# Linear attention in a Trainium2 transformer layer: the normalisation of the query-times-KV product, moved from VectorE to ScalarE and VectorE together

## The chip, the cores and the metric

The kernel runs on all 8 cores of one Trainium2 chip. There are four batch items of 2048 tokens, and each core does one half of one item (1024 tokens). All 8 cores run the same program. The metric is the device time of the slowest core in microseconds (us).

## What is computed

One layer: linear attention with a residual and a layernorm, then a mixture of 8 experts with a residual and a layernorm. The change lies in the attention:

```python
sq = elu_plus_one(q)                                # 16 heads of 128
sk = elu_plus_one(k)                                # 4 KV heads, each repeated for 4 query heads
kv = jnp.einsum('bhsd,bhse->bhde', sk, v)           # 128x128 per head
qkv = jnp.einsum('bhsd,bhde->bhse', sq, kv)
k_sum = sk.sum(axis=2)
norm = jnp.einsum('bhsd,bhd->bhs', sq, k_sum)
attn = qkv / (norm[..., None] + EPS)                # EPS = 1e-6
return attn.transpose(0, 2, 1, 3).reshape(b, s, H * D) @ Wo.T
```

## The kernel before

The program is written by hand, stage by stage. Each stage is one `nc.Block` with a function for each engine. The engines of a block run side by side, ordered only by semaphores that the code names (`wait_ge`, `then_inc`); at the end of a block all engines meet. The stages are: init, kpass (K projection), vpass (V projection and the product of K and V), qproj (Q projection), qkv, wo (output projection), ln1, routerdown, the experts, and then the up projection, the core projection and the last layernorm.

The change touches qkv (lines 583 to 639). It makes 128 tiles, 16 heads by 8 tiles of 128 tokens. For tile i:

- **Q(i)**, TensorE, line 592: a matmul of the 128x128 query tile with `kvaug`, the 128x128 product of K and V with one more column, the sum of K. The result, 128x129 in a PSUM bank `pb[i % 4]`, holds the unnormalised attention in columns 0 to 127 and the norm in column 128.
- **add**, VectorE, line 622: norm + EPS into `rc[4]`, 128x1. It is wrapped in `chain` (line 202), which lets the engine wait for the semaphore of its own instruction.
- **R(i)**, VectorE, line 625: reciprocal into `rc[5]`, 128x1, in `chain` too.
- **M(i)**, VectorE, line 626: columns 0 to 127 times the reciprocal, into `tbx[i % 2]`, bf16.
- **T(i)**, TensorE, line 602 (line 610 for the last two): transpose of `tbx` into `pbf[i % 2]`, the bf16 view of the PSUM bank `pbx`. It waits for M(i), and for the copy C(i-2).
- **C(i)**, VectorE, line 633 (637 for the last): copy of the transposed tile into its place in `arC`, from which wo reads. It waits for one transpose more than its own, so C(i-1) waits for T(i).

The order on TensorE is Q(i+2), T(i), Q(i+3), T(i+1) and so on. The order on VectorE is add(i), R(i), M(i), C(i-1), add(i+1). Semaphore `mma` counts the matmuls, `mmb` the transposes, `dva` the scalings (by two, since a `nop` counts as well), `dvb` the copies and `dvs` the steps of `chain`. ScalarE, GpSimd and SyncE have no work in this stage.

Around it: the stage qproj ends with the epilogues of lines 557 (ScalarE, relu with a per-partition bias from PSUM), 568 (VectorE), 561 (ScalarE, exp) and 572 (VectorE); line 331 is the same relu without a bias, in kpass. Stage wo streams Wo: SyncE issues the loads at line 489, ScalarE casts each piece to bf16 with a Copy activation at line 510, and TensorE multiplies at line 533. The query projection uses the same function and so the same lines. Line 1037 is a Copy activation in the experts, lines 868 and 873 are small activations in the router, lines 722 and 737 are a Square activation and the matmul behind it in ln1. L1282, in a later stage, is a transpose like T.

Of the kernel before, what the change touches and what calls it, by code (L numbers as in the profile page):

```python
# [6 lines left out]
F32 = mybir.dt.float32  # L7
# [55 lines left out]
def build_nc():  # L63
# [43 lines left out]
    def sb(name, shape, dt):  # L107
        return stx.enter_context(nc.sbuf_tensor(name, list(shape), dt))
# [63 lines left out]
    phg = sb("phg", (128, 64), BF16)  # L172
    rbc = sb("rbc", (8, 1), F32)
    ncc = sb("ncc", (8, 1), F32)
    idb = sb("idb", (128, 128), BF16)
    id8 = sb("id8", (8, 8), F32)
    onr = sb("onr", (1, 128), BF16)
# [24 lines left out]
    def chain(eng, instr, ctr):  # L202
        instr.then_inc(ctr.h, 1)
        ctr.add(1)
        eng.wait_ge(ctr.h, ctr.v)  # L205
# [3 lines left out]
    try:  # L209
        with nc.Block("init") as blk:  # L210
# [50 lines left out]
            @blk.vector  # L261
            def _(v):
                v.memset(kvaug[:], 0.0)
                chain(v, v.memset(rc[0][:, 0:1], 1.0), dvs)
                chain(v, v.reciprocal(rc[1][:, 0:1], rc[0][:, 0:1]), dvs)
                chain(v, v.reciprocal(rc[1][:, 0:1], rc[0][:, 0:1]), dvs)
                for jc in range(NJ):
                    v.wait_ge(ldx2[0].h, 16 * (jc + 1))
                    v.tensor_copy(xtb(jc)[:, 0:1024], w2st[0][:, :]
                                  ).then_inc(dvs.h, 1)  # L270
                    dvs.add(1)
                    v.wait_ge(ldx2[1].h, 16 * (jc + 1))
                    v.tensor_copy(xtb(jc)[:, 1024:2048], w2st[1][:, :]
                                  ).then_inc(dvs.h, 1)
                    dvs.add(1)
                v.wait_ge(dvs.h, dvs.v)
                v.nop().then_inc(dva.h, 1)
                dva.add(1)
# [302 lines left out]

        _ck(4)
        with nc.Block("qkv") as blk:
            mma_b, mmb_b, dva_b, dvb_b = mma.v, mmb.v, dva.v, dvb.v

            @blk.tensor
            def _(te):
                for i in range(128):
                    h, ti = i // NT1, i % NT1
                    if i >= 4:  # L590
                        te.wait_ge(dva.h, dva_b + 2 * (i - 4) + 2)
                    te.matmul(pb[i % 4][:, 0:129],
                              sqv(h)[:, ti * 128:(ti + 1) * 128],
                              kvaug[:, (h // 4) * 130:(h // 4) * 130 + 129],
                              start=True, stop=True).then_inc(mma.h, 1)
                    mma.add(1)
                    if i >= 2:
                        k = i - 2
                        te.wait_ge(dva.h, dva_b + 2 * k + 2)
                        if k >= 2:  # L600
                            te.wait_ge(dvb.h, dvb_b + k - 1)
                        te.transpose(pbf[k % 2][:], tbx[k % 2][:, 0:128],  # L602
                                     idb[:]).then_inc(mmb.h, 1)
                        mmb.add(1)
                te.drain().then_inc(mma.h, 1)
                mma.add(1)
                for k in (126, 127):
                    te.wait_ge(dva.h, dva_b + 2 * k + 2)
                    te.wait_ge(dvb.h, dvb_b + k - 1)
                    te.transpose(pbf[k % 2][:], tbx[k % 2][:, 0:128], idb[:]  # L610
                                 ).then_inc(mmb.h, 1)
                    mmb.add(1)
                te.drain().then_inc(mmb.h, 1)
                mmb.add(1)

            @blk.vector
            def _(v):
                for i in range(128):
                    v.wait_ge(mma.h, mma_b + min(i + 3, 129))
                    v.nop().then_inc(dva.h, 1)  # L620
                    dva.add(1)
                    chain(v, v.tensor_scalar(rc[4][:, 0:1],
                                             pb[i % 4][:, 128:129],
                                             EPS_ATTN, None, ALU.add), dvs)
                    chain(v, v.reciprocal(rc[5][:, 0:1], rc[4][:, 0:1]), dvs)
                    v.tensor_scalar(tbx[i % 2][:, 0:128], pb[i % 4][:, 0:128],  # L626
                                    rc[5][:, 0:1], None, ALU.mult).then_inc(dva.h, 1)
                    dva.add(1)
                    if i >= 1:
                        k = i - 1  # L630
                        h, ti = k // NT1, k % NT1
                        v.wait_ge(mmb.h, mmb_b + min(k + 2, 129))
                        v.tensor_copy(atv(h)[:, ti * 128:(ti + 1) * 128],
                                      pbf[k % 2][:]).then_inc(dvb.h, 1)
                        dvb.add(1)
                v.wait_ge(mmb.h, mmb_b + 129)
                v.tensor_copy(atv(15)[:, 7 * 128:8 * 128], pbf[127 % 2][:]
                              ).then_inc(dvb.h, 1)
                dvb.add(1)

        dump("attnT", bfv(arC)[:, 0:16384], (128, 16384), BF16)
        dump("qdbg", stg[:, 0:512], (128, 512), F32)
# [834 lines left out]
```

## Time and profile before

| | us |
|---|---|
| two timed runs | 3197.44 and 3456.91, median 3327.17 |
| profiled execution | 3207.53 |
| its slowest core (core 0), first to last instruction | 3206.0 |
| the other cores of that execution | 3156.3 to 3195.6 |
| busy in the span: TensorE / weight loads / VectorE / ScalarE / GpSimd | 2110.3 / 873.9 / 708.0 / 804.1 / 279.0 |

All 8 cores ran at a mean granted TensorE clock between 0.845 and 0.852 of full speed. Times in the profile are from the start of the span. A "granted clock" of 1.0 is 2.4 GHz, 0.5 is 1.2 GHz. In a view, `[0.62 <-PE pbx L602]` behind an instruction means that its engine sat idle 0.62 us before it, and that the last thing it waited for was TensorE's write to pbx at line 602.

### The profile page before, as it was taken

The numbers are of one execution on the slowest core, as the hardware profiler recorded it, in microseconds if no ns is written. First come the engines' busy times: TensorE is split into PE (matmuls) and PEld (weight loads), VectorE is DVE, ScalarE is ACT, GpSimd is POOL, SyncE is SP. The second block draws the span as 40 slices with busy tenths as digits, with TensorE's granted clock in tenths as the row PEclk, the third lists the DMA queues.
The fourth block names the chain that finished last, engine by engine and source line by source line (L and its number), as shares of the span: only waits on it lengthen the run. The fifth ranks groups of instructions, "written<-read, shape, count | busy, mean of one in ns | idle before, by whom it ended". The sixth has DMA issues, their size and how long they took to land. (4 is left out here: it accounts for less than half of the span.)

```text
span 3206.0 us, 29912 instructions; the slowest of 8 cores (3156.3 to 3206.0 us)
## 1 busy us (share of the span) xinstructions
PE 2110.3 (66%) x8759; PEld 873.9 (27%) x8926; DVE 708.0 (22%) x1553; ACT 804.1 (25%) x1371; POOL 279.0 (9%) x724
## 2 busy tenths in 40 slices
PE   0258673225843708888888888888888887737981
PEld 0023231112300303333333333333333333303420
DVE  2121224551135021111111111111111111230116
ACT  0130441003341232222222222222222222124341
POOL 1000000000000001111111111111111111000000
PEclk9989885557966859899999999999999999858985
DMA  4310330004502113334443333333333333104412
GB/s 153 112 53 1 112 95 4 1 1 143 166 7 59 47 33 116 110 119 124 122 118 114 118 112 106 105 106 105 105 105 106 105 105 124 54 14 136 129 38 105
DMA packets 213226, 287.48 MB, mean 90 GB/s; under 512 B 27713, under 2 KB 179265, under 8 KB 213068
## 3 DMA queue, kind: packets, MB, share of 16 engines
q1 hardware_dynamic: 206156, 260.39, 26.9%
q0 software_dynamic: 6912, 25.17, 2.5%
q8 instruction: 76, 1.25, 0.2%
q14 instruction: 82, 0.67, 0.1%
HBM read 277.08 MB, written 8.39 MB: 89 GB/s over the span
## 5 line engine op out<-in xcount | busy, mean ns | idle before, releaser
L1060 PE MATMUL pb<-arE,wsl 128*128 128x512 bf16 x1771 | 459.5, 412 | 229.1 <-POOL wsl L1011 161.1
L1081 PE MATMUL pb<-arB,arF 128*128 128x512 bf16 x1753 | 403.1, 379 | 27.0 <-ACT arF L1028 25.2
L1011 POOL CAST wsl<-stg 128x256 bf16<-128x256 f32 x672 | 253.5, 400 | 1607.7 <-DMA stg<-w 1420.8
L1142 DVE SCALAR_TENSOR_TENSOR arC<-pb,wgt,arC 128x512 f32<-128x512 f32 x203 | 151.8, 751 | 788.5 <-PE pbx L1081 410.6
L1060 PEld LDWEIGHTS pb<-arE,wsl 128*128 128x128 bf16 x1792 | 181.3, 104 | 493.6 <-issue 327.2
L1028 ACT ACTIVATE arF<-pb,b1all 128x512 bf16<-128x512 f32 x224 | 151.5, 682 | 644.8 <-PE pbx L1060 331.9
L1060 PE MATMUL pbx<-arE,wsl 128*128 128x512 bf16 x861 | 232.8, 413 | 73.9 <-POOL wsl L1011 37.3
L1081 PEld LDWEIGHTS pb<-arB,arF 128*128 128x128 bf16 x1792 | 174.2, 98 | 238.7 <-issue 30.5
L1037 ACT ACTIVATE arB<-w2st 128x1024 bf16<-128x1024 f32 x168 | 176.7, 1052 | 175.3 <-DMA w2st<-w 169.0
L1081 PE MATMUL pbx<-arB,arF 128*128 128x512 bf16 x879 | 209.4, 379 | 12.9 <-ACT arF L1028 12.0
L1028 ACT ACTIVATE arF<-pbx,b1all 128x512 bf16<-128x512 f32 x112 | 76.5, 683 | 345.6 <-PE pb L1060 336.1
L533 PE MATMUL pb<-arA,wsl 128*128 128x512 bf16 x501 | 126.3, 415 | 54.9 <-DVE arB L572 38.1
L1142 DVE SCALAR_TENSOR_TENSOR arC<-pbx,wgt,arC 128x512 f32<-128x512 f32 x101 | 75.8, 751 | 369.9 <-PE pb L1081 364.0
L1373 PE MATMUL pb<-arC,wsl 128*128 128x512 bf16 x500 | 122.9, 398 | 51.8 <-ACT wsl L1335 39.9
L349 PE MATMUL pb<-wsl,arA 128*128 128x512 bf16 x251 | 59.6, 389 | 140.8 <-ACT wsl L324 140.6
L1060 PEld LDWEIGHTS pbx<-arE,wsl 128*128 128x128 bf16 x896 | 91.1, 104 | 204.4 <-issue 121.2
L602 PE MATMUL pbx<-idb,tb 128*128 128x128 bf16 x126 | 33.5, 266 | 171.7 <-DVE tb L626 171.7
L533 PE MATMUL pb<-arC,wsl 128*128 128x512 bf16 x501 | 116.4, 392 | 38.0 <-ACT wsl L510 36.2
L510 ACT ACTIVATE wsl<-stg 128x256 bf16<-128x256 f32 x256 | 98.6, 413 | 125.2 <-DMA stg<-wot 78.5
L1081 PEld LDWEIGHTS pbx<-arB,arF 128*128 128x128 bf16 x896 | 87.1, 98 | 119.4 <-issue 15.3
L533 PEld LDWEIGHTS pb<-arA,wsl 128*128 128x128 bf16 x512 | 53.3, 105 | 127.6 <-issue 78.3
L1373 PEld LDWEIGHTS pb<-arC,wsl 128*128 128x128 bf16 x512 | 51.7, 102 | 118.4 <-issue 64.4
(152 smaller groups left out, 1539.7 us busy)
## 6 DMA issues: line engine op xcount, KB each, us to landing
stg<-w SPq DMA_DIRECT2D x640, 128.0 KB, 3.6
w2st<-w SPq DMA_DIRECT2D x160, 512.0 KB, 4.8
w2st<-xt POOLq DMA_DIRECT2D x48, 512.0 KB, 4.8
stg<-wqt SPq DMA_DIRECT2D x128, 128.0 KB, 2.5
stg<-wot SPq DMA_DIRECT2D x128, 128.0 KB, 3.0
stg<-core_w SPq DMA_DIRECT2D x128, 128.0 KB, 2.6
stg<-down_w SPq DMA_DIRECT2D x64, 128.0 KB, 2.5
w2st<-up_w SPq DMA_DIRECT2D x64, 128.0 KB, 2.5
```

The costliest lines, as they stand in the source:

```text
L349: te.matmul(pb[s_ % 4][:, 0:512], xtb(jc)[:, s_ * 128:(s_ + 1) * 128], wslv(jc // 8)[:, (jc % 8) * 512:(jc % 8) * 512 + 512], start=(jc == ...
L510: sc.activation(wslv(osl % 2)[:, ic * 256:(ic + 1) * 256], stgv(np_), AF.Copy).then_inc(aca.h, 1)
L533: mm = te.matmul(pb[i % 4][:, 0:512], wslv(osl % 2)[:, ic * 256 + k2 * 128: ic * 256 + k2 * 128 + 128], rhs_fn(ic, th), start=(ic == 0), s ...
L602: te.transpose(pbf[k % 2][:], tbx[k % 2][:, 0:128], idb[:]).then_inc(mmb.h, 1)
L1011: gp.tensor_copy(wslv(sg % 2)[:, lc * 256:(lc + 1) * 256], stgv(npiece)).then_inc(gpc.h, 1)
L1028: sc.activation(Uv(hcl)[:, th * 512:th * 512 + 512], eb1[ztg % 3][:], AF.Gelu, bias=b1all[:, bcol:bcol + 1]).then_inc(acb.h, 1)
L1037: sc.activation(w2g(zt)[:, :], w2st[kc % 2][:, :], AF.Copy).then_inc(aca.h, 1)
L1060: mm = te.matmul(eb1[ztg % 3][:, 0:512], wslv(sg % 2)[:, lc * 256 + k2 * 128: lc * 256 + k2 * 128 + 128], gTv(lc)[:, th * 512:th * 512 + 512],
L1081: mm = te.matmul(eb2[mtg % 3][:, 0:512], Uv(hcl)[:, ti * 128:(ti + 1) * 128], w2g(hcl)[:, lh * 512:lh * 512 + 512], start=(hcl == 0), stop ...
L1142: fl = v.scalar_tensor_tensor(dst, eb2[mtg % 3][:], wgt[:, ti * 8 + g["e"]: ti * 8 + g["e"] + 1], dst, ALU.mult, ALU.add)
L1373: te.matmul(pb[i % 4][:, 0:512], wslv(osl % 2)[:, jc * 256 + k2 * 128: jc * 256 + k2 * 128 + 128], gx2v(jc)[:, th * 512:th * 512 + 512], s ...
```

## The change

In qkv the add of EPS and the scaling M move from VectorE to ScalarE, as Copy activations: the add with EPS as an immediate bias, M with the reciprocal as a per-partition scale. The reciprocal stays on VectorE.

- ScalarE's order is N(i), M(i-1), N(i+1), M(i) and so on, where N is the add. N(i) waits for matmul Q(i+1) and then for R(i-2), whose input buffer it overwrites. M(k) waits for transpose T(k-2) and then for R(k).
- VectorE's order is R(i), C(i-1), R(i+1), C(i). R(i) waits for N(i) and then for M(i-2), whose scale it overwrites. The self-waits of `chain` and the `nop` are gone.
- `rc[4]` and `rc[5]` (sums) and `rc[2]` and `rc[3]` (reciprocals) are each used in turn.
- TensorE does what it did; it waits for the scaling on `acb` (ScalarE) in place of `dva`.
- The last copy becomes part of the loop. A 128x1 constant `epsc` is set in init and is not read.

```diff
@@ -172,6 +172,7 @@
     phg = sb("phg", (128, 64), BF16)
     rbc = sb("rbc", (8, 1), F32)
     ncc = sb("ncc", (8, 1), F32)
+    epsc = sb("epsc", (128, 1), F32)
     idb = sb("idb", (128, 128), BF16)
     id8 = sb("id8", (8, 8), F32)
     onr = sb("onr", (1, 128), BF16)
@@ -261,6 +262,7 @@
             @blk.vector
             def _(v):
                 v.memset(kvaug[:], 0.0)
+                v.memset(epsc[:, 0:1], EPS_ATTN)
                 chain(v, v.memset(rc[0][:, 0:1], 1.0), dvs)
                 chain(v, v.reciprocal(rc[1][:, 0:1], rc[0][:, 0:1]), dvs)
                 chain(v, v.reciprocal(rc[1][:, 0:1], rc[0][:, 0:1]), dvs)
@@ -581,14 +583,14 @@
 
         _ck(4)
         with nc.Block("qkv") as blk:
-            mma_b, mmb_b, dva_b, dvb_b = mma.v, mmb.v, dva.v, dvb.v
+            mma_b, mmb_b, dvb_b, acb_b = mma.v, mmb.v, dvb.v, acb.v
 
             @blk.tensor
             def _(te):
                 for i in range(128):
                     h, ti = i // NT1, i % NT1
                     if i >= 4:
-                        te.wait_ge(dva.h, dva_b + 2 * (i - 4) + 2)
+                        te.wait_ge(acb.h, acb_b + (i - 4) + 1)
                     te.matmul(pb[i % 4][:, 0:129],
                               sqv(h)[:, ti * 128:(ti + 1) * 128],
                               kvaug[:, (h // 4) * 130:(h // 4) * 130 + 129],
@@ -596,7 +598,7 @@
                     mma.add(1)
                     if i >= 2:
                         k = i - 2
-                        te.wait_ge(dva.h, dva_b + 2 * k + 2)
+                        te.wait_ge(acb.h, acb_b + k + 1)
                         if k >= 2:
                             te.wait_ge(dvb.h, dvb_b + k - 1)
                         te.transpose(pbf[k % 2][:], tbx[k % 2][:, 0:128],
@@ -605,7 +607,7 @@
                 te.drain().then_inc(mma.h, 1)
                 mma.add(1)
                 for k in (126, 127):
-                    te.wait_ge(dva.h, dva_b + 2 * k + 2)
+                    te.wait_ge(acb.h, acb_b + k + 1)
                     te.wait_ge(dvb.h, dvb_b + k - 1)
                     te.transpose(pbf[k % 2][:], tbx[k % 2][:, 0:128], idb[:]
                                  ).then_inc(mmb.h, 1)
@@ -613,19 +615,40 @@
                 te.drain().then_inc(mmb.h, 1)
                 mmb.add(1)
 
+            acs_b, dva_b = acs.v, dva.v
+
+            @blk.scalar
+            def _(sc):
+                for i in range(129):
+                    if i < 128:
+                        sc.wait_ge(mma.h, mma_b + min(i + 2, 129))
+                        if i >= 2:
+                            sc.wait_ge(dva.h, dva_b + i - 1)
+                        sc.activation(rc[4 + i % 2][:, 0:1],
+                                      pb[i % 4][:, 128:129], AF.Copy,
+                                      bias=EPS_ATTN).then_inc(acs.h, 1)
+                        acs.add(1)
+                    if i >= 1:
+                        k = i - 1
+                        if k >= 2:
+                            sc.wait_ge(mmb.h, mmb_b + k - 1)
+                        sc.wait_ge(dva.h, dva_b + k + 1)
+                        sc.activation(tbx[k % 2][:, 0:128],
+                                      pb[k % 4][:, 0:128],
+                                      AF.Copy, scale=rc[2 + k % 2][:, 0:1]
+                                      ).then_inc(acb.h, 1)
+                        acb.add(1)
+
             @blk.vector
             def _(v):
-                for i in range(128):
-                    v.wait_ge(mma.h, mma_b + min(i + 3, 129))
-                    v.nop().then_inc(dva.h, 1)
-                    dva.add(1)
-                    chain(v, v.tensor_scalar(rc[4][:, 0:1],
-                                             pb[i % 4][:, 128:129],
-                                             EPS_ATTN, None, ALU.add), dvs)
-                    chain(v, v.reciprocal(rc[5][:, 0:1], rc[4][:, 0:1]), dvs)
-                    v.tensor_scalar(tbx[i % 2][:, 0:128], pb[i % 4][:, 0:128],
-                                    rc[5][:, 0:1], None, ALU.mult).then_inc(dva.h, 1)
-                    dva.add(1)
+                for i in range(129):
+                    if i < 128:
+                        v.wait_ge(acs.h, acs_b + i + 1)
+                        if i >= 2:
+                            v.wait_ge(acb.h, acb_b + i - 1)
+                        v.reciprocal(rc[2 + i % 2][:, 0:1],
+                                     rc[4 + i % 2][:, 0:1]).then_inc(dva.h, 1)
+                        dva.add(1)
                     if i >= 1:
                         k = i - 1
                         h, ti = k // NT1, k % NT1
@@ -633,10 +656,6 @@
                         v.tensor_copy(atv(h)[:, ti * 128:(ti + 1) * 128],
                                       pbf[k % 2][:]).then_inc(dvb.h, 1)
                         dvb.add(1)
-                v.wait_ge(mmb.h, mmb_b + 129)
-                v.tensor_copy(atv(15)[:, 7 * 128:8 * 128], pbf[127 % 2][:]
-                              ).then_inc(dvb.h, 1)
-                dvb.add(1)
 
         dump("attnT", bfv(arC)[:, 0:16384], (128, 16384), BF16)
         dump("qdbg", stg[:, 0:512], (128, 512), F32)
```

## Rows read from the trace of the kernel before

**Rows 1.** The page: the span, and the TensorE clock granted in 40 slices.
```profile
span 3206.0 us, 29912 instructions; the slowest of 8 cores (3156.3 to 3206.0 us)
...
PEclk9989885557966859899999999999999999858985
```

**Rows 2.** Stretches, core 0: us, busy PE, PEld, DVE, ACT, POOL, granted clock, DMA.
```profile
512.00:734.00 222.00, 49.63 (x251) 25.96 (x250) 113.25 (x505) 0.00 (x0) 0.00 (x0) 0.50 0.00 1
737.00:760.00 23.00, 3.88 (x12) 1.68 (x14) 0.00 (x0) 9.80 (x23) 0.55 (x2) 0.52 0.61 178
2817.00:2864.00 47.00, 16.84 (x64) 6.61 (x64) 18.87 (x78) 0.00 (x0) 0.00 (x0) 0.50 0.00 1
```

**Rows 3.** Waits of SyncE's queue, 500 to 745 us: total, times, longest.
```profile
SPq L583 <- PEq L583: 226.0, 1, 226.0
```

**Rows 4.** Timeline, one tile of qkv: start us, us, engine, line, operation, idle before.
```profile
603.67 0.23 DVE L633 COPY arC<-pbx 128x128 bf16<-128x128 bf16 x1 [0.62 <-PE pbx L602]
603.89 0.16 DVE L622 TENSOR_SCALAR rc<-pb 128x1 f32<-128x1 f32 x1
604.16 0.16 DVE L625 RECIPROCAL rc<-rc 128x1 f32<-128x1 f32 x1
604.43 0.35 DVE L626 TENSOR_SCALAR tb<-pb,rc 128x128 bf16<-128x128 f32 x1
605.00 0.10 PEld L602 LDWEIGHTS pbx<-idb,tb 128*128 128x128 bf16 x1 [1.50 <-issue]
605.03 0.27 PE L602 MATMUL pbx<-idb,tb 128*128 128x128 bf16 x1 [1.34 <-DVE tb L626]
...
605.16 0.27 PE L592 MATMUL pb<-kvaug,arB 128*128 128x129 bf16 x1
605.40 0.23 DVE L633 COPY arC<-pbx 128x128 bf16<-128x128 bf16 x1 [0.62 <-PE pbx L602]
```

**Rows 5.** Timeline, the first tile of qkv.
```profile
511.14 0.35 DVE L626 TENSOR_SCALAR tb<-pb,rc 128x128 bf16<-128x128 f32 x1
511.61 0.10 PEld L602 LDWEIGHTS pbx<-idb,tb 128*128 128x128 bf16 x1 [1.48 <-issue]
```

**Rows 6.** Timeline, the end of qkv and the start of wo.
```profile
734.94 0.10 PEld L610 LDWEIGHTS pbx<-idb,tb 128*128 128x128 bf16 x1 [1.60 <-issue]
...
735.97 9.17 SPq L489 DMA_DIRECT2D stg<-wot  x8
...
738.37 1.28 ACT L510 ACT_TABLE_LOAD   x1 [229.57 <-DMA stg<-wot]
```

**Rows 7.** Groups of ScalarE: line, operation, shapes, count, busy us, mean ns, idle before.
```profile
L1037 ACT ACTIVATE arB<-w2st 128x1024 bf16<-128x1024 f32 x168 | 176.7, 1052 | 175.3 <-DMA w2st<-w 169.0 <-DMA w2st<-shared_w 6.3
...
L510 ACT ACTIVATE wsl<-stg 128x256 bf16<-128x256 f32 x256 | 98.6, 413 | 125.2 <-DMA stg<-wot 78.5 <-DMA stg<-wqt 40.1 <-PE pb L533 3.7
...
L557 ACT ACTIVATE tscr<-pb,bqs 128x512 f32<-128x512 f32 x32 | 21.6, 675 | 20.2 <-PE pb L533 19.0 <-PEq L545 1.2
...
L331 ACT ACTIVATE tscr<-pb 128x512 f32<-128x512 f32 x16 | 9.5, 596 | 34.7 <-PE pb L353 32.9 <-PEq L358 1.8
L510 ACT ACT_TABLE_LOAD x2 | 2.6, 1283 | 317.3 <-DMA stg<-wot 229.6 <-DMA stg<-wqt 87.7
...
L868 ACT ACTIVATE rt<-rt,rc 128x8 f32<-128x8 f32 x8 | 2.4, 300 | 0.1
...
L873 ACT ACTIVATE rc<-rc 128x1 f32<-128x1 f32 x8 | 1.5, 186 | 0.0
```

**Rows 8.** Timeline, query projection: ScalarE waits for VectorE.
```profile
501.69 0.75 DVE L568 TENSOR_SCALAR tscr<-pb,bqs 128x512 f32<-128x512 f32 x1 [1.19 <-ACT tscr L557]
502.54 0.63 ACT L561 ACTIVATE tscr<-tscr 128x512 f32<-128x512 f32 x1 [0.95 <-DVE tscr L568]
```

**Rows 9.** Timeline, first layernorm: TensorE waits for ScalarE.
```profile
895.68 0.61 ACT L722 ACTIVATE tscr<-arA 128x512 bf16<-128x512 f32 x1
...
896.41 0.08 PEld L737 LDWEIGHTS pb<-tb,onc 128*1 128x1 bf16 x1 [1.31 <-issue]
```

## The prediction

> **What bounds the kernel now.** I read the page first. The core shown ends at 3206.0 us, and in slices 7 to 9 of 40 (80 us each) the granted TensorE clock is 0.5 of full speed [rows 1]. That is the stage called qkv. The view of stretches says what happens there: from 512 to 734 us VectorE is busy 113 of 222 us, TensorE 50, ScalarE and GpSimd nothing, no data is loaded, and the clock stands at 0.50, the 1.2 GHz level [rows 2]. No engine is full, so something must go round in a ring.
>
> Next, is the stage joined to its neighbours, or closed? The queue of SyncE, which loads the next stage's weights, stands 226.0 us at the end-of-stage synchronisation of qkv (line 583) [rows 3]. The first load of Wo is issued at 735.97, 1.0 us after the last transpose has begun [rows 6]. Nothing of wo is done ahead, so each microsecond taken from qkv should leave the whole kernel. (The whole-kernel chain of waits is no help, as it only follows the end.)
>
> Now one tile in the timeline [rows 4]. The reader should see the following ring, in us from the start of the copy at 603.67:
>
> - copy C of an older transpose, VectorE, 0.225, with the add of EPS starting as it ends (603.89);
> - the add takes 0.16, but the reciprocal starts 0.27 after the add did, since it waits 0.10 for its own engine's semaphore;
> - the scaling starts 0.27 after the reciprocal and takes 0.35, to 604.78;
> - the weight load of the transpose T starts 0.22 later (605.00);
> - the next copy starts 0.40 after that weight load (605.40).
>
> The sum is 0.22 + 0.27 + 0.27 + 0.35 + 0.22 + 0.40 = 1.73 us, and C to C is 605.40 - 603.67 = 1.73. The matmul Q, issued behind T at 605.16, is not in the ring. The first transpose loads at 511.61 [rows 5], the last at 734.94 [rows 6]: 223.3 us for 127 steps, or 1.758 each. 127 steps of 1.73 are 219.7, so 3.6 us are irregular stalls, which I leave in.
>
> **The change part by part.**
>
> *The EPS constant in init.* One 128x1 memset, which nothing reads. In init VectorE waits for the DMA of x; the cost is nil, and some 0.1 us even without that cover.
>
> *The add moves to ScalarE (call it N).* N(i+2) reads the bank of Q(i+3), which TensorE issues right behind T(i). So the add runs beside the copy, one to two tiles ahead of the scaling it serves. VectorE's chain loses the add and the self-wait: 0.27.
>
> *The scaling moves to ScalarE (M).* Its duration there has no row, so from neighbours [rows 7]: a PSUM read of 512 columns takes 596 ns without a pointer operand (line 331) and 675 with one (line 557). The slope is (1052 - 413)/768 = 0.832 ns per column. 128 columns with a pointer are 675 - 384 x 0.832 = 355 ns, against 0.35 on VectorE: no gain and no loss. For N, 596 - 511 x 0.832 = 171 ns; the 128x1 row of line 873 has 186. I take 0.18. The bounds: M at 0.28 if the pointer is free (596 - 384 x 0.832) and 0.40 if all PSUM savings vanish; N from 0.17 to 0.30 (line 868, 128x8 with a pointer).
>
> A rule of the Trainium skill speaks against both moves: page "ScalarE: Activation LUTs", section "Rules for kernel authors", says to do adds and multiplies on VectorE and not on ScalarE. The rows do not bear it out for this shape, since 0.355 stands against 0.35. By that page's section "What ACT_TABLE_LOAD costs" (186 ns, 93 for a pointer operand, 0.833 per column) M would be 0.386, an estimate; the ring below would then be 1.49 and the time some 4 us higher than mine.
>
> *The hand-overs.* VectorE to ScalarE: line 568 ends at 501.69 + 0.75 = 502.44 and line 561 starts at 502.54, so 0.10 [rows 8]. ScalarE to TensorE: line 722 ends at 896.29 and the weight load starts at 896.41, so 0.12 [rows 9]. VectorE to TensorE in qkv is 0.12 for the first tile, too (511.49 to 511.61) [rows 5], and 0.22 in the steady state [rows 4], where T waits for two semaphores (from k = 2 on). The new code keeps the two waits in the same order, so I take 0.22.
>
> *The new ring A:* M(i) 0.355, to TensorE 0.22, T to C(i-1) 0.40, C 0.225, reciprocal R(i+1) 0.16 directly behind it, to ScalarE 0.10, M(i+1). Sum 1.46. R's two waits (N(i+1), M(i-1)) are over by then, and so is M's wait for T(i-1).
>
> *The new ring B:* M(i) 0.355, to TensorE 0.22, T and Q(i+3) to the end of Q 0.43 (605.00 to 605.16 + 0.27), to ScalarE 0.20 (two waits, the late one first: 0.10 more, as for T), N(i+2) 0.18, and M(i+1) directly behind it on ScalarE. Sum 1.385. N(i+2) is over 0.08 before R(i+1) lets M go, so ring A sets the pace, narrowly.
>
> *Queued behind the waits.* On VectorE R(i+1) stands behind C(i-1), on ScalarE M(i+1) behind N(i+2), on TensorE Q(i+3) behind T(i); all are in the two rings. No DMA queue is touched.
>
> *ScalarE's first activation of the stage.* ScalarE does nothing in qkv now. Each of the two stages that use line 510 begins with a table load of 1.28 us (256 activations in all, but only 2 loads) [rows 7]. The wo stage keeps its load (738.37) [rows 6]. qkv gets one more. Two matmuls are done about 510.3 (the first three end by 510.40, a little before VectorE begins), the table is there at 511.7, then N 0.18, hop 0.10, R 0.16, hop 0.10, M 0.355, hop 0.12: first T at about 512.7 in place of 511.61 [rows 5]. That costs 1.1.
>
> The same skill page and section count another 1.38 us of drain to each switch of table. No row here isolates it; by it the start would cost 2.5.
>
> *The end.* The last copy is now one of the loop's, waiting for the same drain: nil.
>
> *Sum.* 127 steps x (1.73 - 1.46) = 34.3 saved, 1.1 paid: 33 us. The profiled execution took 3207.53 us (span 3206.0 and 1.5 around it), so 3207.5 - 33 = 3174.5, rounded to 3175. The two timed runs were 3197.44 and 3456.91, a median of 3327.17; the profiled execution stands 10 us above the first and far below the median, which is the midpoint of two runs 8% apart. My number is for an execution like the profiled one. From 3197.44 the same sum gives 3164.
>
> **The rivals.**
>
> *ScalarE becomes the bound (ring B).* With N at 0.30 and 0.10 more between N and M, because M has two waits of its own, ring B is 1.385 + 0.12 + 0.10 = 1.605. Saved: 127 x 0.125 = 16, less 1.1: 3193. For it: ring B lies only 0.08 below A, and ScalarE now has two instructions and four waits per tile. Against: consecutive activations without a hand-over have idle 0.0 between them (line 873) [rows 7].
>
> *The steps are shorter than I think.* M at 0.28 and T free of its second wait's 0.10: ring A 1.29, but ring B then 1.385 - 0.075 - 0.10 = 1.21, so 1.29: 127 x 0.44 = 56, less 1.1: 3153. Each alone gives 9 to 13 us more than my sum. The clock could rise to its 2.4 GHz level as TensorE gets denser (50/222 = 23% busy now, 50/189 = 26% then). Against: from 2817 to 2864 us the same transposes ran at 16.84/47 = 36% busy with the clock at 0.50 throughout [rows 2].
>
> *It does not reach the end.* If wo could not start earlier, because something other than qkv gates it, the time is 3207 to 3209. Against: the loads wait at the stage's end and start right behind it [rows 3, 6]. wo runs at the 0.52 clock from 737 to 760 whenever it begins [rows 2].
>
> *Slower: a table load at more than the first activation.* Should ScalarE reload its table within the loop, each load lies in ring A or B at 1.28. The gain of 33 is gone from 26 loads on, and one per tile gives 127 x 1.28 = 163 more, 3338. For it: ScalarE has never run such an instruction pair here. Against: both activations use one function, and line 510's 256 activations, alternated in the query projection with two other functions, show 2 loads.
>
> **How the numbers follow.** Ring A as summed (3165 to 3185): 0.62. Ring B or dearer hand-overs (3185 to 3203): 0.19. Shorter steps (3145 to 3165): 0.11. No effect: 0.05. Slower by reloads: 0.03. The predicted time is that of the first, 3175. The range is 3145 to 3212: it reaches down to the short bound less the 10 us by which an execution may lie below the profiled one, and up to no effect. 2% of 3207 is 64 us, about what a measurement of this kernel can tell from no change. A gain of 64 needs a step of 1.22, below both rings: 0.03. Slower by over 2% needs the reloads: 0.04 with what I have not thought of. Within 2%: 0.93.
>
> **What would show it.** In the changed profile: qkv from its first transpose to its last 127 x 1.46 + 3.6 = 189 us, not 223; the steady step 1.46; M about 0.355 and N about 0.18; M started by the reciprocal (ring A) and not directly at N's end (ring B); one table load at about 510.3; clock 0.50; Wo's first load at about 703. I am wrong if M's releaser is N or if the step lies outside 1.39 to 1.60, or if the stretch is shorter but the stages behind it longer.

## The result, and the profile after

The changed kernel takes 0.9898 of the time of the kernel before (95% interval 0.9864 to 0.9933). Executions in which a whole die runs at a lower clock are left out on both sides, here and below. Of 3207 us that is 33 us less, and the interval runs from 21 to 44. Its profiled execution took 3202.04 us.

The page of the changed kernel, its span and its granted clock by slice:

```profile
span 3200.5 us, 30331 instructions; the slowest of 8 cores (3111.0 to 3200.5 us)
...
PEclk9989886559868769779999999999999977858985
```

The span is only 5.5 us shorter than before [rows 1], because the slowest core of this execution lost time elsewhere. The first row below is core 0 of the kernel before, the second core 1 of the changed kernel, each from its first to its last expert matmul. The columns are those of rows 2.

```profile
1195.00:2783.00 1588.00, 1318.63 (x5584) 560.28 (x5696) 253.88 (x372) 388.67 (x505) 250.43 (x664) 0.94 0.37 110
```

```profile
1161.30:2786.00 1624.70, 1372.99 (x5695) 571.62 (x5696) 253.92 (x372) 388.61 (x505) 250.23 (x664) 0.91 0.35 108
```

The experts' code is the same, and so is the busy time of VectorE and ScalarE, but this stretch ran at a clock of 0.91 in place of 0.94 and took 1624.7 us in place of 1588.0. That is 37 us in a stretch in which no line was changed. Over all 8 cores it did not grow: its median was 1573.6 us before and is 1572.1 now. What is left of a core's span without it had a median of 1613.3 us and has 1574.8, 38.5 less, and the median of the 8 whole spans went from 3188.9 to 3145.2 us. So I read the stage itself, and its length from the first to the last transpose is the number to go by. It was 223.2 to 223.3 us on the 8 cores before, and is 182.7 to 183.1 now.

One tile of qkv in the changed kernel, timeline. L656 is the copy C, L649 the reciprocal R, L627 the add N on ScalarE, L636 the scaling M on ScalarE, L604 the transpose T and L594 the matmul Q:

```profile
602.11 0.22 DVE L656 COPY arC<-pbx 128x128 bf16<-128x128 bf16 x1 [1.08 <-PE pbx L604]
602.28 0.17 ACT L627 ACTIVATE rc<-pb 128x1 f32<-128x1 f32 x1 [0.79 <-PE pb L594]
602.29 0.16 DVE L649 RECIPROCAL rc<-rc 128x1 f32<-128x1 f32 x1
602.54 0.37 ACT L636 ACTIVATE tb<-pb,rc 128x128 bf16<-128x128 f32 x1
603.13 0.10 PEld L604 LDWEIGHTS pbx<-idb,tb 128*128 128x128 bf16 x1 [1.19 <-issue]
...
603.26 0.10 PEld L594 LDWEIGHTS pb<-kvaug,arB 128*128 128x128 bf16 x1
603.29 0.27 PE L594 MATMUL pb<-kvaug,arB 128*128 128x129 bf16 x1
603.53 0.22 DVE L656 COPY arC<-pbx 128x128 bf16<-128x128 bf16 x1 [1.08 <-PE pbx L604]
```

Set beside [rows 4], the ring now runs copy (602.11), reciprocal (602.29), scaling (602.54), weight load of the transpose (603.13), next copy (603.53): 0.18 + 0.25 + 0.59 + 0.40 = 1.42 us. The add (602.28) runs at the same time as the reciprocal of another tile, and the ring no longer contains it.

The stage without its start and end, columns as in rows 2, and its largest waits between 530 and 690 us, columns as in rows 3:

```profile
520.00:700.00 180.00, 49.42 (x250) 25.76 (x250) 41.72 (x248) 67.15 (x251) 0.00 (x0) 0.50 0.00 1
```

```profile
DVE arC L656 <- PE pbx L604: 122.1, 111, 1.4
PE pbx L604 <- ACT tb L636: 116.1, 111, 1.4
ACT rc L627 <- PE pb L594: 88.1, 110, 0.9
```

VectorE is busy a quarter of the time, and waits for a transpose; TensorE waits for the scaling; ScalarE's adds wait for a matmul. It is still a ring, with no full engine, at the 0.50 clock [rows 2].

The start of the stage (against rows 5) and its end (against rows 6):

```profile
518.63 1.28 ACT L627 ACT_TABLE_LOAD   x1 [1.57 <-PE pb L594]
519.92 0.23 ACT L627 ACTIVATE rc<-pb 128x1 f32<-128x1 f32 x2
520.20 0.26 DVE L649 RECIPROCAL rc<-rc 128x1 f32<-128x1 f32 x2 [2.35 <-ACT rc L627]
520.46 0.37 ACT L636 ACTIVATE tb<-pb,rc 128x128 bf16<-128x128 f32 x1 [0.30 <-DVE rc L649]
520.94 0.10 PEld L604 LDWEIGHTS pbx<-idb,tb 128*128 128x128 bf16 x1 [2.55 <-issue]
```

```profile
703.95 0.10 PEld L612 LDWEIGHTS pbx<-idb,tb 128*128 128x128 bf16 x1 [1.32 <-issue]
...
704.99 7.18 SPq L491 DMA_DIRECT2D stg<-wot  x7
...
707.27 1.28 ACT L512 ACT_TABLE_LOAD   x1 [3.54 <-DMA stg<-wot]
```

One table load comes before the first add. The first transpose follows the stage's first matmul by 2.8 us in place of 1.7. At the end, the loads for wo begin 1.0 us after the last transpose, as before.

### The profile page after: what moved, and what is told of

Read it like the earlier page. It is cut to its first block and busy times, and to the rows that moved or that the text cites. A ratio compares the mean times of both kernels' runs of the same rounds, so it can differ in the third digit from the quotient of the medians.

```text
span 3200.5 us, 30331 instructions; the slowest of 8 cores (3111.0 to 3200.5 us)
## 1 busy us (share of the span) xinstructions
PE 2157.9 (67%) x8926; PEld 883.4 (28%) x8926; DVE 636.4 (20%) x1298; ACT 873.7 (27%) x1628; POOL 278.8 (9%) x724
## 3 DMA queue, kind: packets, MB, share of 16 engines
q8 instruction: 76, 1.25, 0.2%
## 5 line engine op out<-in xcount | busy, mean ns | idle before, releaser
L1079 PE MATMUL pb<-arE,wsl 128*128 128x512 bf16 x1792 | 469.0, 418 | 213.1 <-POOL wsl L1030 153.8
L1100 PE MATMUL pb<-arB,arF 128*128 128x512 bf16 x1792 | 425.2, 392 | 24.0 <-ACT arF L1047 24.0
L1079 PE MATMUL pbx<-arE,wsl 128*128 128x512 bf16 x896 | 245.4, 424 | 75.2 <-POOL wsl L1030 38.5
L1100 PE MATMUL pbx<-arB,arF 128*128 128x512 bf16 x896 | 220.9, 391 | 12.0 <-ACT arF L1047 12.0
L351 PE MATMUL pb<-wsl,arA 128*128 128x512 bf16 x256 | 60.7, 392 | 144.3 <-ACT wsl L326 144.3
L604 PE MATMUL pbx<-idb,tb 128*128 128x128 bf16 x126 | 33.5, 266 | 132.9 <-ACT tb L636 132.9
L422 PE MATMUL pb<-wsl,arA 128*128 128x512 bf16 x256 | 60.3, 390 | 34.7 <-ACT wsl L409 34.7
```

What stands on the lines that cost most here:

```text
L351: te.matmul(pb[s_ % 4][:, 0:512], xtb(jc)[:, s_ * 128:(s_ + 1) * 128], wslv(jc // 8)[:, (jc % 8) * 512:(jc % 8) * 512 + 512], start=(jc == ...
L422: te.matmul(pb[s_ % 4][:, 0:512], xtb(jc)[:, s_ * 128:(s_ + 1) * 128], wslv(jc // 8)[:, (jc % 8) * 512:(jc % 8) * 512 + 512], start=(jc == ...
L604: te.transpose(pbf[k % 2][:], tbx[k % 2][:, 0:128], idb[:]).then_inc(mmb.h, 1)
L1079: mm = te.matmul(eb1[ztg % 3][:, 0:512], wslv(sg % 2)[:, lc * 256 + k2 * 128: lc * 256 + k2 * 128 + 128], gTv(lc)[:, th * 512:th * 512 + 512],
L1100: mm = te.matmul(eb2[mtg % 3][:, 0:512], Uv(hcl)[:, ti * 128:(ti + 1) * 128], w2g(hcl)[:, lh * 512:lh * 512 + 512], start=(hcl == 0), stop ...
```

## The experiments

All lengths below are from the first to the last transpose of the stage (127 steps), in us. The cores of one execution differ by 0.5 at most; the median core is given. "Step" is the median time from one transpose to the next. In e8 the steps swing, so their mean is given there.

| kernel | first to last transpose | step |
|---|---|---|
| before | 223.3 | 1.73 |
| changed | 183.0 | 1.42 |
| e1, e11: only the add on ScalarE | 176.5 | 1.38 |
| e2: only the scaling on ScalarE | 215.1 | 1.68 |
| e3: before, without the nop | 208.8 | 1.64 |
| e4: changed, waits of the transpose in the other order | 169.1 | 1.31 |
| e5: changed, reciprocal ahead of the copy | 167.6 | 1.31 |
| e6: changed, one more activation per tile | 183.3 | 1.42 |
| e7: changed, three more | 184.1 | 1.42 |
| e9: changed, one wait at the reciprocal | 178.1 | 1.38 |
| e10: only the add, and waits as in e4 | 162.5 | 1.27 |
| e8: changed, deeper | 77.8 | 0.61 |
| e12: only the add, deeper | 70.6 | 0.53 |

### Each half of the change alone (e1, e2)

For e1, the scaling stays on VectorE and ScalarE only adds:

```diff
+                for i in range(128):
+                    sc.wait_ge(mma.h, mma_b + min(i + 2, 129))
+                    if i >= 2:
+                        sc.wait_ge(dvs.h, dvs_b + i - 1)
+                    sc.activation(rc[4 + i % 2][:, 0:1],
+                                  pb[i % 4][:, 128:129], AF.Copy,
+                                  bias=EPS_ATTN).then_inc(acs.h, 1)
...
                         v.wait_ge(acs.h, acs_b + i + 1)
-                        if i >= 2:
-                            v.wait_ge(acb.h, acb_b + i - 1)
-                        v.reciprocal(rc[2 + i % 2][:, 0:1],
-                                     rc[4 + i % 2][:, 0:1]).then_inc(dva.h, 1)
+                        chain(v, v.reciprocal(rc[2 + i % 2][:, 0:1],
+                                              rc[4 + i % 2][:, 0:1]), dvs)
+                        v.tensor_scalar(tbx[i % 2][:, 0:128],
+                                        pb[i % 4][:, 0:128],
+                                        rc[2 + i % 2][:, 0:1], None,
+                                        ALU.mult).then_inc(dva.h, 1)
```

> Only the add of EPS moves to ScalarE; reciprocal and scaling stay on VectorE. My theory (ring A: the gain is the add and its self-wait leaving VectorE's chain, and nothing comes from the scaling): the step is reciprocal 0.16 + self-wait 0.11 + scaling 0.35 + 0.22 + 0.40 + copy 0.18 to 0.225 = 1.42 to 1.47 us, so 183 to 189 us from the first transpose to the last, like the changed kernel's 183.0. Rival (the gain comes from sharing the work between two engines, VectorE being relieved of the scaling too): 1.55 or more, over 199 us.

Measured: 176.5, below what I expected and 6.5 less than with the whole change. Only the stage is read here; e11 times the whole kernel. The timeline of e1, with L647 the copy, L636 the reciprocal, L626 the add and L638 the scaling:

```profile
600.32 0.23 DVE L647 COPY arC<-pbx 128x128 bf16<-128x128 bf16 x1 [0.62 <-PE pbx L604]
600.46 0.15 DVE L636 RECIPROCAL rc<-rc 128x1 f32<-128x1 f32 x1
600.49 0.17 ACT L626 ACTIVATE rc<-pb 128x1 f32<-128x1 f32 x1 [1.21 <-PE pb L594]
600.72 0.35 DVE L638 TENSOR_SCALAR tb<-pb,rc 128x128 bf16<-128x128 f32 x1
601.29 0.11 PEld L604 LDWEIGHTS pbx<-idb,tb 128*128 128x128 bf16 x1 [1.15 <-issue]
```

The reciprocal starts 0.14 after the copy, not 0.18. The rest is as it was: 0.26 to the scaling, 0.57 to the transpose, 0.40 to the next copy (601.69), in all 1.37.

For e2 it is the other way round, add and reciprocal on VectorE:

```diff
+                for k in range(128):
+                    if k >= 2:
+                        sc.wait_ge(mmb.h, mmb_b + k - 1)
+                    sc.wait_ge(dva.h, dva_b + k + 1)
+                    sc.activation(tbx[k % 2][:, 0:128],
+                                  pb[k % 4][:, 0:128],
+                                  AF.Copy, scale=rc[2 + k % 2][:, 0:1]
+                                  ).then_inc(acb.h, 1)
...
                         if i >= 2:
                             v.wait_ge(acb.h, acb_b + i - 1)
+                        chain(v, v.tensor_scalar(rc[4 + i % 2][:, 0:1],
+                                                 pb[i % 4][:, 128:129],
+                                                 EPS_ATTN, None, ALU.add), dvs)
                         v.reciprocal(rc[2 + i % 2][:, 0:1],
```

> Only the scaling moves to ScalarE; add and reciprocal stay on VectorE. My theory: copy 0.18 to 0.225, add 0.16 + self-wait 0.11, reciprocal 0.16 + 0.09 to ScalarE, scaling 0.37, 0.22, 0.40 = 1.59 to 1.64 us if the copy no longer holds up its follower, 203 to 210 us from first to last transpose: most of the old 223. Rival (sharing the work is what counts): near 1.45, under 190 us.

Measured: 215.1. The sum on record was added up wrongly, as its own terms make 0.18 + 0.27 + 0.25 + 0.37 + 0.22 + 0.40 = 1.69. The rows (L649 the copy, L639 the add, L642 the reciprocal, L626 the scaling) agree with that:

```profile
599.93 0.23 DVE L649 COPY arC<-pbx 128x128 bf16<-128x128 bf16 x1 [1.08 <-PE pbx L604]
600.11 0.16 DVE L639 TENSOR_SCALAR rc<-pb 128x1 f32<-128x1 f32 x1
600.37 0.16 DVE L642 RECIPROCAL rc<-rc 128x1 f32<-128x1 f32 x1
600.63 0.37 ACT L626 ACTIVATE tb<-pb,rc 128x128 bf16<-128x128 f32 x1 [1.32 <-DVE rc L642]
601.22 0.10 PEld L604 LDWEIGHTS pbx<-idb,tb 128*128 128x128 bf16 x1 [1.46 <-issue]
```

From copy to add 0.18, to the reciprocal 0.26, to the scaling 0.26, to the transpose 0.59. The stage is 8 us shorter than before, but e2 has no nop either, and that alone brings 14.5 (e3, next). Against e3 the scaling costs 6.3.

### The nop (e3)

```diff
                     v.wait_ge(mma.h, mma_b + min(i + 3, 129))
-                    v.nop().then_inc(dva.h, 1)
-                    dva.add(1)
                     chain(v, v.tensor_scalar(rc[4][:, 0:1],
```

The waits on `dva` count one per tile in place of two.

> The kernel before, without the nop that VectorE runs between its wait for the matmul and the add; the scaling's count goes up by one per tile in place of two. In the changed kernel the reciprocal starts 0.18 us after the copy does, in the old one the add started 0.225 after it. Theory: the nop ahead of the add is what kept it from starting early; without it the step is 1.69 (0.045 less), 217.5 us in place of 223.3. Rival: the early start belongs to the kind of instruction (an SBUF reciprocal against a PSUM add), then 223.3 stays.

Measured: 208.8, so 14.5 less than before with no work moved at all, and more than I expected. Timeline, L631 the copy, L620 the add, L623 the reciprocal:

```profile
600.13 0.22 DVE L631 COPY arC<-pbx 128x128 bf16<-128x128 bf16 x1 [0.62 <-PE pbx L602]
600.27 0.15 DVE L620 TENSOR_SCALAR rc<-pb 128x1 f32<-128x1 f32 x1
600.52 0.16 DVE L623 RECIPROCAL rc<-rc 128x1 f32<-128x1 f32 x1
```

The add starts 0.14 after the copy does, before the copy's reported end, where it started 0.22 after it in [rows 4]. The rival, that this depends on the kind of instruction, falls: this is the same PSUM add. The median step is 0.096 shorter, 12.2 us over 127 steps. The other 2.3 are irregular stalls, of which there are fewer: the length less 127 median steps is 3.1 us before and 0.8 here. Why, no run shows.

The trace of the kernel before already held the 0.14. Its last two copies have one wait and no nop between them:

```profile
735.35 0.23 DVE L633 COPY arC<-pbx 128x128 bf16<-128x128 bf16 x1 [0.62 <-PEq L613]
735.49 0.21 DVE L637 COPY arC<-pbx 128x128 bf16<-128x128 bf16 x1
```

### The waits of the reciprocal (e9)

```diff
-                                      bias=EPS_ATTN).then_inc(acs.h, 1)
+                                      bias=EPS_ATTN).then_inc(acb.h, 1)
...
-                        v.wait_ge(acs.h, acs_b + i + 1)
-                        if i >= 2:
-                            v.wait_ge(acb.h, acb_b + i - 1)
+                        v.wait_ge(acb.h, acb_b + max(2 * i, 1))
                         v.reciprocal(rc[2 + i % 2][:, 0:1],
```

TensorE's waits on `acb` are counted anew, so that each is still for the same scaling.

> The changed kernel with ScalarE's adds and scalings counted on one semaphore, so that the reciprocal waits once in place of twice; the order of all work is the same. Theory: an instruction starts 0.14 us after the start of the copy ahead of it when it has one wait between them (the kernel with only the add moved, and the one without the nop), 0.18 when it has two, 0.225 with a wait, a nop and a second instruction. So the step falls from 1.42 to 1.38, and first to last transpose from 183 to 178 us. Rival: 0.18 belongs to ScalarE's part in the ring; then 183 stays.

Measured: 178.1. L654 is the copy, L647 the reciprocal:

```profile
561.43 0.22 DVE L654 COPY arC<-pbx 128x128 bf16<-128x128 bf16 x1 [1.12 <-PE pbx L604]
561.57 0.15 DVE L647 RECIPROCAL rc<-rc 128x1 f32<-128x1 f32 x1
```

From the start of this copy to the start of the instruction behind it takes 0.14 with one wait between them, 0.17 to 0.18 with two, and 0.22 to 0.23 with the wait and the nop. Both waits are over long before, so what costs is that VectorE has to get through them. This gives 4.9 of the 6.5 us by which the whole change is behind e1. The other 1.6 I leave to the scaling's 0.368 against 0.351 and to small differences of the hand-overs, which I did not separate.

### The waits of the transpose (e4, e10)

```diff
-                        te.wait_ge(acb.h, acb_b + k + 1)
                         if k >= 2:
                             te.wait_ge(dvb.h, dvb_b + k - 1)
+                        te.wait_ge(acb.h, acb_b + k + 1)
                         te.transpose(pbf[k % 2][:], tbx[k % 2][:, 0:128],
```

> The changed kernel with the transpose's two waits in the other order: first the copy of two tiles before, which is long over, then the scaling, which comes last. Theory: 0.10 of the 0.22 us between the scaling and the transpose's weight load is the second wait's own turn behind the late first one, so the hop becomes 0.12, the step 1.32, and first to last transpose 170 us in place of 183. Rival: the hop is 0.22 because TensorE is slow to start a transpose in the steady state; then 183 stays.

Measured: 169.1. The scaling (L636) and the weight load of the transpose:

```profile
600.79 0.37 ACT L636 ACTIVATE tb<-pb,rc 128x128 bf16<-128x128 f32 x1
601.27 0.10 PEld L604 LDWEIGHTS pbx<-idb,tb 128*128 128x128 bf16 x1 [0.97 <-issue]
```

The scaling ends at 601.16 and the weight load starts 0.11 later, in place of 0.22. The last two transposes, in their own loop, were changed alike. The order in which two waits are written is worth 13.9 us here. With only the add moved it brings as much:

> Only the add moves to ScalarE, and the transpose's two waits change places. Theory: the gains add: the kernel with only the add moved has 176.5 us, less 127 x 0.10 for the order of the waits, is 163.8; the step is 1.27. Beside the kernel before that is 59.5 less in the stage and 1.1 more ahead of it, 58 us, a ratio of 0.982. Rival (something else is right behind the ring): over 170.

Measured: 162.5, step 1.27. The median times were 3144.9 us for e10 and 3205.0 for the kernel before beside it, which is 0.981; with three executions against two I give no interval.

> Only the add moves to ScalarE, timed in rounds, since a single execution before said little of the whole kernel. Theory: the stage takes 176.5 us from first to last transpose in place of 223.3, and starts 1.1 later, so 45.7 less, a ratio of 0.986; the changed kernel had 0.990 with 40.3 less. Rival (what VectorE keeps costs elsewhere): 0.995 or more.

Measured: 176.5 again, and a median of 3160.7 us over four executions, 0.986 of the same 3205.0, where 0.986 was expected. That it is better than the whole change rests on the 6.5 us in the stage; the whole times alone could not tell the two apart.

### Which ring sets the step (e5, e6, e7)

```diff
-                for i in range(129):
+                for i in range(130):
...
-                    if i >= 1:
-                        k = i - 1
+                    if i >= 2:
+                        k = i - 2
```

In e5, the second `if` on VectorE (the copy) so follows the reciprocal of two tiles on, in place of one.

> The changed kernel with VectorE's order turned round: R(i+1) ahead of C(i-1). That cuts ring A (scaling, transpose, copy, reciprocal, scaling) and leaves ring B (scaling, transpose, matmul, add on ScalarE, scaling). Theory: ring A set the step at 1.42; ring B by the changed kernel's rows is 0.37 + 0.22 + 0.43 + 0.14 + 0.09 = 1.25, so 127 x 1.25 + 2.7 = 161 us from first to last transpose. Rival (ScalarE and ring B set the step already): 183 stays.

Measured: 167.6, a step of 1.31, so ring A did set the step, and with it cut the step falls by 0.11 and no further. The rows are ring B (L594 the matmul, L627 the add, L636 the scaling):

```profile
600.18 0.37 ACT L636 ACTIVATE tb<-pb,rc 128x128 bf16<-128x128 f32 x1
...
600.77 0.10 PEld L604 LDWEIGHTS pbx<-idb,tb 128*128 128x128 bf16 x1 [1.07 <-issue]
...
600.92 0.27 PE L594 MATMUL pb<-kvaug,arB 128*128 128x129 bf16 x1
...
601.34 0.17 ACT L627 ACTIVATE rc<-pb 128x1 f32<-128x1 f32 x1 [0.80 <-PE pb L594]
601.49 0.37 ACT L636 ACTIVATE tb<-pb,rc 128x128 bf16<-128x128 f32 x1
```

Scaling to weight load 0.59, to the end of the matmul (600.92 + 0.27) 0.42, to the add 0.15, to the next scaling 0.15. That is 1.31; I had 1.25, from an add and a scaling 0.09 apart.

e6 and e7 lengthen ring B in place of cutting ring A. This is e7; e6 has one activation in place of three:

```diff
+                        for j in range(3):
+                            sc.activation(stg[:, 3 * i + j:3 * i + j + 1],
+                                          pb[i % 4][:, 128:129], AF.Copy,
+                                          bias=EPS_ATTN)
                         sc.activation(rc[4 + i % 2][:, 0:1],
```

> The changed kernel with one useless activation of 128x1 ahead of each add on ScalarE. Theory: ring B has 1.42 - 1.25 = 0.17 us to spare and two small activations start 0.09 apart, so nothing changes: 183 us from first to last transpose. Rival (ring B sets the step): 0.09 to 0.17 more per tile, 194 to 205 us.

Measured: 183.3 against 183.0, and the same step, so ring B has room to spare.

> Three useless activations of 128x1 ahead of each add on ScalarE. Theory: ring B becomes 1.25 + 3 x 0.09 = 1.52 and takes over from ring A at 1.42: 127 x 1.52 + 2.7 = 196 us. If each costs its whole 0.17 in place of 0.09, 1.76 and 226 us. Rival (ScalarE is far off the path): 183 stays.

Measured: 184.1, where I expected 196. The reciprocal (L653), the three idle adds in one row (L628), the real add (L631) and the scaling (L640):

```profile
602.72 0.16 DVE L653 RECIPROCAL rc<-rc 128x1 f32<-128x1 f32 x1
602.72 0.30 ACT L628 ACTIVATE stg<-pb 128x1 f32<-128x1 f32 x3 [0.80 <-PE pb L594]
602.89 0.19 ACT L631 ACTIVATE rc<-pb 128x1 f32<-128x1 f32 x1
602.97 0.37 ACT L640 ACTIVATE tb<-pb,rc 128x128 bf16<-128x128 f32 x1
```

Three additional activations move the real add by 0.17, that is 0.06 each, though each has 0.17 of busy time. The add then starts at 602.89 and the scaling 0.08 behind it, just when the reciprocal (602.72 + 0.16) lets it go: the point where ring B takes over is reached and not passed. By e5, ring B had only 0.11 to spare. It takes in the 0.17 because the scaling now starts 0.08 behind the add, where it started 0.15 behind it in e5: by the trace, ScalarE has here gone through the first of the scaling's two waits before the real add starts.

### A longer ring (e8, e12)

Both rings exist because each tile waits for its neighbour. e8 gives every step more distance:

```diff
+            pt = pbf + [pb[4].bitcast(BF16)[:, 0:128],
+                        pb[5].bitcast(BF16)[:, 0:128]]
+            tq = lambda k: tbx[k % 2][:, (k // 2 % 2) * 128:
+                                      (k // 2 % 2) * 128 + 128]
...
-                    if i >= 2:
-                        k = i - 2
+                    if i >= 3:
+                        k = i - 3
+                        if k >= 4:
+                            te.wait_ge(dvb.h, dvb_b + k - 3)
                         te.wait_ge(acb.h, acb_b + k + 1)
-                        if k >= 2:
-                            te.wait_ge(dvb.h, dvb_b + k - 1)
-                        te.transpose(pbf[k % 2][:], tbx[k % 2][:, 0:128],
-                                     idb[:]).then_inc(mmb.h, 1)
+                        te.transpose(pt[k % 4][:], tq(k), idb[:]
+                                     ).then_inc(mmb.h, 1)
...
-                        if k >= 2:
-                            sc.wait_ge(mmb.h, mmb_b + k - 1)
+                        if k >= 4:
+                            sc.wait_ge(mmb.h, mmb_b + k - 3)
```

> The changed kernel with more distance between the steps: transposes go to four PSUM banks in place of two and wait for the copy of four tiles before, the scaled tile has four places in place of two, the transpose T(k) is issued behind matmul Q(k+3) in place of Q(k+2), the copy C(k) stands behind reciprocal R(k+3), and the transpose's late wait comes last. Theory: both rings then span two or three tiles. Ring B: (0.37 + 0.12 + 0.43 + 0.14 + 0.09)/2 = 0.57 us a tile, ring A (0.37 + 0.12 + 0.40 + 0.18 + 0.16 + 0.09)/3 = 0.44, ScalarE's own work 0.36 to 0.54. So 0.57 to 0.65, 72 to 85 us from first to last transpose, about 105 us less than the changed kernel, and 4 to 5% under the kernel before. Rival (shared buffers or PSUM access of three engines keep a floor of about 1 us a tile): 130 us, 3% under the kernel before.

Measured: 77.8 us for the stage, and for the kernel a ratio of 0.9534 (95% interval 0.9507 to 0.9561), 150 us less than the kernel before (141 to 158). Both kernels under study are beaten, and the whole of the stage's 145.5 us, less the 1.1 at the start, arrives at the end. Of the stage's gain over the changed kernel, 105 us, the order of the transpose's waits brings 13.9 by itself (e4); what the extra buffers and the extra distance bring one by one was not separated. 60 us of the stage, columns as in rows 2:

```profile
530.00:590.00 60.00, 38.52 (x195) 20.13 (x194) 34.54 (x196) 47.24 (x196) 0.00 (x0) 0.50 0.01 2
```

ScalarE is now the busiest, at 47 of 60 us, but not full. What sets this kernel's step was not shown.

In e12, the scaling goes back to VectorE, whose order is then R(i), C(i-3), M(i):

```diff
+                    if i < 128:
+                        if i >= 4:
+                            v.wait_ge(mmb.h, mmb_b + i - 3)
+                        v.wait_ge(dvs.h, dvs_b + i + 1)
+                        v.tensor_scalar(tq(i), pb[i % 4][:, 0:128],
+                                        rc[2 + i % 2][:, 0:1], None,
+                                        ALU.mult).then_inc(dva.h, 1)
```

> The deeper kernel, but with the scaling back on VectorE, so that only the add is on ScalarE; VectorE's order is R(i), C(i-3), M(i). Theory: once the ring is long, the busiest engine sets the pace. VectorE has 0.16 + 0.225 + 0.35 = 0.74 us a tile in place of ScalarE's 0.37 + 0.17 = 0.54, so the step is 0.70 to 0.80 and first to last transpose 89 to 102 us, in place of 76.9: here moving the scaling pays. Rival (the pace is set by the hand-overs, not by an engine): 77 or less, as VectorE's scaling saves a hand-over.

Measured: 70.6, and my theory fell. I expected moving the scaling to pay at last; it still costs 7.2 us. (The 76.9 on record for the deeper kernel ends two transposes early; to the last one it is 77.8.) The four executions took 3054.4 to 3060.8 us, median 3056.6, which is 0.954 of the 3205.0 beside it, with only two executions of before to compare with. The same 60 us, and one tile on VectorE in the timeline (L640 the reciprocal, L647 the copy, L654 the scaling):

```profile
530.00:590.00 60.00, 42.98 (x218) 22.64 (x217) 58.51 (x328) 18.52 (x108) 0.00 (x0) 0.50 0.01 2
```

```profile
561.63 0.15 DVE L640 RECIPROCAL rc<-rc 128x1 f32<-128x1 f32 x1
561.72 0.23 DVE L647 COPY arC<-pb 128x128 bf16<-128x128 bf16 x1
...
561.90 0.35 DVE L654 TENSOR_SCALAR tb<-pb,rc 128x128 bf16<-128x128 f32 x1
...
562.17 0.15 DVE L640 RECIPROCAL rc<-rc 128x1 f32<-128x1 f32 x1
```

VectorE is the bound as I had said, at 58.5 of 60 us, but a tile costs it 0.54 (561.63 to 562.17) and not the 0.74 that its durations add up to: the copy starts 0.09 after the reciprocal, the scaling 0.18 after the copy, the next reciprocal 0.27 after the scaling. Where nothing is waited for, the reported durations overlap. Stalls bring the mean step to 0.56.

## Why the prediction was right, and where it was off

The prediction was 3175 us, against 3202 for the profiled execution and 33 us (21 to 44) of gain by the ratio; it forecast 33. That the two agree to the microsecond is luck. The stage gave 6 us more than forecast, from terms that were off in both directions, and the interval is 11 us wide on either side. An interval of that width also tells apart far less than the 64 us that the prediction names.

- **The stage is a closed ring, and all of its gain reaches the end.** Right. It became 39.2 shorter (40.3, less 1.1 at the start), within the interval of the ratio, and the spans without the experts 38.5. Better shown by e8: 145.5 less in the stage, 150 less in the kernel.
- **The add leaves the ring, the scaling brings nothing.** Right for the add. For the scaling it was a loss: e1 has all of the gain and 6.5 more. 4.9 of the 6.5 is the second wait that the reciprocal has to make because ScalarE reads its result (e9). I had taken both of its waits as over and so as free. The scaling's duration I had set at 0.355 on ScalarE against 0.35; it is 0.368 against 0.351.
- **Ring A 1.46 and ring B 1.385.** The order was right (the scaling is released by the reciprocal; e5, e6), the sizes were not: 1.42 and 1.31 (e5). In ring A the term mis-sized is "C 0.225, reciprocal directly behind it". I took it from [rows 4], where the add started as the copy ended, and did not see that this was the cost of the nop there. It is 0.18. This 0.045 x 127 is 5.7 us, about the 6 us between the forecast 189 and 183.0. In ring B, the add took 0.18 from start to scaling in my sum and takes 0.15, and the hand-over from the matmul 0.20 and takes 0.15. The prediction also says that N(i+2) reads the bank of Q(i+3). It reads that of Q(i+2), and waits for the matmul after it. That wait is what puts Q(i+3) into ring B.
- **What the add's removal is worth.** I put 0.27 on the add and its self-wait and nothing on the nop. By e3 the nop alone is 14.5 us. From there to e1 the add brings 32.3 (208.8 - 176.5), against 127 x 0.27 = 34.3 forecast, and moving the scaling takes 6.5 back, which makes the 40.3. I had listed the instruction in the kernel and left it out of the sum, because the views count it as no work.
- **0.22 to TensorE because of two waits.** Right, and e4 confirms the cause: 0.11 with the late wait last.
- **The start, 1.1.** Right: 1.1 (from the first matmul to the first transpose 2.76, in place of 1.69). The first add starts 0.01 after the table load ends (518.63 + 1.28 against 519.92). The Trainium skill's 1.38 us of drain beside each switch of table set ("ScalarE: Activation LUTs", section "What ACT_TABLE_LOAD costs") does not appear here, where ScalarE was idle before. By the figures that the Trainium skill gives in the same section the scaling would take 0.386, an estimate, against 0.368 measured with a PSUM source.
- **The Trainium skill's rule against the move** ("ScalarE: Activation LUTs", "Rules for kernel authors": adds and multiplies belong on VectorE, for its rate per element). For the multiply the runs agree with it, by 6.5 us here and 7.2 in the deeper kernel, though most of the 6.5 is a wait and not ScalarE's speed. For the add they do not: e1 is 32.3 us shorter than e3, which has no nop either, because its place beside the ring counts and not its duration.
- **Rivals.** Ring B as the bound: no, it takes three more activations to reach it (e7). Steps shorter than summed: true for one term of ring A, the copy, and not for the two that the rival names; the order of the waits could have been one of them (e4). No effect: the gain arrives. A reload per tile: one load is seen in the stage. The clock stayed at 0.50 throughout.

## What to carry over

Where no engine is full, write down the ring from one row of the timeline to the next, start to start, and include what the busy times do not count: here a nop was worth 14.5 us, one more satisfied wait 4.9, and putting the late wait last 13.9. In this stage, work taken off the ring paid, and work handed from one engine on the ring to another did not, though the second was idle. Before shifting work at all, ask whether the ring can be made to span more tiles: with four buffers in place of two, one or two tiles more of distance and the late wait last, the stage fell from 223 to 71 or 78 us, over three and a half times the gain of the change.

## What the runs showed of the hardware

- VectorE begins an instruction before the reported end of the one before it. Behind a copy of 0.225 it began 0.14 after the copy's start with one satisfied wait between them (e3, e9), 0.18 with two, and only at its end, 0.22 to 0.23, with a wait and a nop. With one satisfied wait, it was 0.09 behind a reciprocal of 0.15, and 0.27 behind a scaling of 0.35 (e12). ScalarE does so with small activations: about 0.06 from start to start at 0.17 of duration each (e7).
- On TensorE, a second wait behind a late first one costs 0.11 (e4).
- In e12, the granted clock was 0.99 from 505.0 to 520.7 us, where the query projection ends and TensorE then stands idle for 5.66 us. From there to the stage's end it stayed at 0.50, the 1.2 GHz level, with TensorE busy 43 of 60 us.
